# Start stage of a two-layer adaptive FFN kernel: factor merges in six groups, eight zero products, x loads by SyncE, lists reordered

## The reference, cut to what matters

```python
hidden_i = jnp.einsum('bsd,fd->bsf', x, wi)
hidden_i += ALPHA * jnp.einsum('bsr,fr->bsf', jnp.einsum('bsd,rd->bsr', x, common_wi_a), common_wi_b)
hidden_i += _expert_lora(x, expert_ids, experts_wi_a, experts_wi_b)
hidden_i = jax.nn.relu(hidden_i)
hidden_o = jnp.einsum('bsf,df->bsd', hidden_i, wo)
...
for r in range(R):                       # four rounds, R = 4
    logits = flat @ Wg[r] + bg[r]        # top 2 of 4 experts, softmax weights cw
    hmid = jax.nn.gelu(jnp.einsum('nh,ehf->enf', flat, W1) + b1[:, None, :])
    y = jnp.einsum('enf,efh->enh', hmid, W2) + b2[:, None, :]
    cur = cur + jnp.einsum('ne,enh->nh', cw, y).reshape(b, s, h)
x = x + ...
```

## Time and profile before

| what | us |
|---|---|
| median of 3 runs (485.28 to 486.13) | 485.58 |
| the profiled execution | 486.61 |
| its span, first to last instruction | 484.80 |
| its mean granted TensorE clock, as a share of full speed | 0.996 |

### The profile page before, as it was taken

The page is one execution under the profiler, slowest core; times in us unless marked ns, Lnnn a source line. Parts: engine busy times, 40 slices in busy tenths (PEclk is TensorE's granted clock), DMA queues, the critical chain, the costliest instruction groups (busy, mean ns, idle before and its releaser), DMA issues.

```text
span 484.8 us, 7478 instructions
## 1 busy us (share of the span) xinstructions
PE 477.9 (99%) x2270; PEld 397.0 (82%) x2270; DVE 387.7 (80%) x641; ACT 393.9 (81%) x542; POOL 118.7 (24%) x102
## 2 busy tenths in 40 slices
PE   7999999999999999999999999999999999999997
PEld 7998888888888888888888888888888887888885
DVE  4789899999879898988898898889897758554343
ACT  3799988888888888988888888888888888697653
POOL 5796212121212112121222121231313144400000
PEclk9999999999999999999999999999999999999999
DMA  7702702020201102020202012120202000000001
GB/s 209 215 5 88 266 18 89 2 87 3 87 11 76 71 16 87 0 87 0 87 0 87 11 76 82 49 89 0 87 2 87 2 0 0 1 0 1 0 22 69
DMA packets 6986, 26.30 MB, mean 54 GB/s; under 512 B 2226, under 2 KB 2610, under 8 KB 4786
## 3 DMA queue, kind: packets, MB, share of 16 engines
q1 hardware_dynamic: 5826, 21.20, 12.1%
q0 software_dynamic: 528, 3.67, 2.2%
q10 hardware_dynamic: 608, 1.11, 0.8%
HBM read 24.81 MB, written 1.18 MB: 54 GB/s over the span
## 4 chain that ended last, share of the span: by engine, by line
PE 96%; DMA 2%; SPq 1%; issue 0%; DVE 0%
PE bank L505 34%; PE bank L506 34%; PE bank L509 26%; DMA stage<-lora_all 2%; PE bank L594 1%; PE bank L595 1%; PE bank L527 1%; SPq L244 0%; SPq L247 0%; PE bank L540 0%; PE bank L524 0%; SPq L257 0%; DVE x L1276 0%; SPq L345 0%; SPq L344 0%
## 5 line engine op out<-in xcount | busy, mean ns | idle before, releaser
L812 ACT ACTIVATE act_out<-bank,vec 128x512 f32<-128x512 f32 x256 | 165.4, 682 | 41.8 <-PE bank L509 32.6
L1115 DVE TENSOR_TENSOR hid_lo<-act_out,hid_hi 128x1024 fp32r<-128x1024 f32 x128 | 156.6, 1243 | 33.3 <-ACT hid_hi L817 33.2
L817 ACT ACTIVATE hid_hi<-act_out 128x1024 fp32r<-128x1024 f32 x128 | 135.9, 1062 | 8.0 <-PE bank L509 0.2
L468 POOL TENSOR_TENSOR cur<-cur,prod 128x512 f32<-128x512 f32 x48 | 64.9, 1352 | 238.4 <-DVE prod L1126 237.9
L505 PE MATMUL bank<-hid_hi,moe_hi 128*128 128x512 f32 x256 | 99.9, 390 | 0.0
L509 PE MATMUL bank<-hid_hi,moe_lo 128*128 128x512 f32 x256 | 99.7, 390 | 0.0
L505 PE MATMUL bank<-xhi,moe_hi 128*128 128x512 f32 x256 | 99.7, 390 | 0.0
L506 PE MATMUL bank<-hid_lo,moe_hi 128*128 128x512 f32 x256 | 99.7, 389 | 0.0
L506 PE MATMUL bank<-xlo,moe_hi 128*128 128x512 f32 x256 | 99.6, 389 | 0.0
L509 PE MATMUL bank<-xhi,moe_lo 128*128 128x512 f32 x256 | 99.6, 389 | 0.0
L505 PEld LDWEIGHTS bank<-hid_hi,moe_hi 128*128 128x128 f32 x256 | 48.1, 188 | 11.3 <-issue 0.2
(11 more groups left out here) (126 smaller groups left out, 569.9 us busy)
## 6 DMA issues: line engine op xcount, KB each, us to landing
cw_all<-cw_dram SPq DMA_DIRECT2D x16, 1024.0 KB, 4.6
stage<-ffn_w POOLq DMA_DIRECT2D x1, 2304.0 KB, 8.5
cw_all<-moe_w SPq DMA_DIRECT2D x4, 512.0 KB, 10.3
stage<-lora_all SPq DMA_DIRECT2D x5, 160.0 KB, 7.1
x<-x_t POOLq DMA_DIRECT2D x3, 256.0 KB, 7.0
out_t<-x SPq DMA_DIRECT2D x3, 256.0 KB, 2.5
cur<-cond_base ACTq DMA_DIRECT2D x2, 256.0 KB, 3.1
stage<-ffn_w POOLq DMA_DIRECT2D x1, 512.0 KB, 3.8
```

Of the source, the lines that this page charges most:

```text
L468: pool.tensor_tensor(cur[:, c, :], cur[:, c, :], prod[:, s % 2, :], ALU.add).then_inc(add_done, 1)
L812: act.activation(act_out[:, f // 2, f % 2, :], bank[:, f, :], ACT.Gelu_apprx_tanh, bias=vec[:, V_B1 + e * FC + f:V_B1 + e * FC + f + 1]).t ...
L817: act.activation(hid_hi[:, s % 2, 2 * pr:2 * pr + 2, :], act_out[:, pr, :, :], ACT.Copy)\
L1115: dve.tensor_tensor(hid_lo[:, s % 2, 2 * pr:2 * pr + 2, :], act_out[:, pr, :, :], hid_hi[:, s % 2, 2 * pr:2 * pr + 2, :].bitcast(F32), ALU ...
```

## The change

Nothing that is computed changes. Seven things do:

1. The 16 merges stand in six groups instead of seven: sizes 2, 2, 3, 3, 3, 3 instead of 2, 2, 2, 2, 3, 3, 2. All groups behind the second use banks 5 to 7; banks 2 and 3 are no longer used for merges.
2. `KEEP_WARM` is 8 instead of 2.
3. x chunks 1, 2 and 3 are issued by SP instead of POOL: chunk 1 behind the factors of batch 2, chunks 2 and 3 behind those of batch 7, ahead of `moe_w`.
4. The sum, high part and low part of merge (0, 0) are made in two halves of 256 columns, with semaphores of their own, and `cond_hidden(0)` waits for each half.
5. The low parts of conditioned chunks 2 and 3 are made by POOL from `cur` instead of by DVE from PSUM; `cond_out(6)` waits for the copy of chunk 2 only.
6. `split_gate` and `x0_low(2)` move from DVE to POOL.
7. The lists of PE, ACT, DVE and POOL stand in a new order.

```diff
 MERGE_GROUPS = (((0, 0), (1, 0)),
                 ((0, 1), (1, 1)),
-                ((2, 0), (3, 0)),
-                ((2, 1), (3, 1)),
-                ((4, 0), (5, 0), (4, 1)),
-                ((6, 0), (7, 0), (5, 1)),
-                ((6, 1), (7, 1)))
+                ((2, 0), (3, 0), (2, 1)),
+                ((4, 0), (5, 0), (3, 1)),
+                ((6, 0), (4, 1), (5, 1)),
+                ((7, 0), (6, 1), (7, 1)))
-MERGE_BANKS = (6, 7, 4, 5, 2, 3, 6, 7, 5, 6, 7, 5, 6, 7, 5, 6)
+MERGE_BANKS = (6, 7, 5, 4, 6, 7, 5, 6, 7, 5, 6, 7, 5, 6, 7, 5)
-WARM, KEEP_WARM = 13, 2
+WARM, KEEP_WARM = 13, 8
             expert_load(sp, 2, expert)
+            x_load(sp, 1)
             for b in (4, 5, 6, 7):
                 lora_load(sp, b)
+            x_load(sp, 2)
+            x_load(sp, 3)
...
-            pool.wait_ge(first_out_in[1], 16)
-            for c in range(1, CHUNKS):
-                x_load(pool, c)
+            def conditioned_low(c):
+                pool.wait_ge(cond_cur, c + 1)
+                pool.tensor_tensor(xlo[:, c, :], cur[:, c, :], xhi[:, c, :].bitcast(F32), ALU.subtract)\
+                    .then_inc(xs_done, 1)
...
                 for f in range(FC):
+                    if b == 0 and f % 2 == 0:
+                        pe.wait_ge(first_lo_done, f // 2 + 1)
...
                     pe.wait_ge(merge_free, summed_in(COND, len(MERGED)))
+                elif b == PER_CHUNK * (CHUNKS - 1):
+                    pe.wait_ge(cond_cur, c)
                 elif b % PER_CHUNK == 0:
                     pe.wait_ge(xs_done, c)
...
             merge_group(2)
-            merge_group(3)
             cond_hidden(0)
             cond_hidden(1)
-            merge_group(4)
+            merge_group(3)
             cond_out(0)
             cond_hidden(2)
-            merge_group(5)
+            merge_group(4)
             cond_out(1)
             cond_hidden(3)
             cond_hidden(4)
-            merge_group(6)
+            merge_group(5)
             cond_out(2)
             cond_out(3)
+            cond_hidden(5)
             first_logits(0)
-            cond_hidden(5)
             cond_hidden(6)
             cond_out(4)
             cond_out(5)
+            cond_hidden(7)
+            cond_out(6)
+            expert_in(0, 0, 0, (0,))
             first_logits(1)
...
+            def first_sum():
+
+                dve.wait_ge(base_in[0], 16)
+                dve.wait_ge(merge_done, MERGED.index((0, 0)) + 1)
+                for half, summed in zip(halves, (first_sum_done, merge_free)):
+                    dve.scalar_tensor_tensor(merged(0, 0)[:, half], bank[:, merge_bank(MERGED.index((0, 0))), half], COND_ALPHA,
+                                             base[:, 0, half], ALU.mult, ALU.add).then_inc(summed, 1)
```

More of the change, by code:

```diff
@@ L219, in adaln_ffn @@
         out_done = sem("out_done")
+        halves = [slice(0, F // 2), slice(F // 2, F)]
         block = ctx.enter_context(nc.Block())
@@ L447, in _ @@
             merged_low(6, 1)
+            moe_low(0)
+            merged_low(7, 1)
             moe_low(4)
-            merged_low(7, 1)
             moe_low(1)
@@ L452, in _ @@
             moe_low(2)
+            pool.wait_ge(cond_cur, CHUNKS)
+            for i in range(2):
+                pool.memset(prod[:, i, 0:1], 0.0).then_inc(add_done, 1)
             moe_low(6)
+            conditioned_low(2)
             moe_low(3)
+            conditioned_low(3)
             moe_low(7)
@@ L697, in _ @@
             cond_out(5)
+            cond_hidden(7)
+            cond_out(6)
+            expert_in(0, 0, 0, (0,))
             first_logits(1)
-            cond_hidden(7)
-            expert_in(0, 0, 0, (0,))
             expert_in(0, 0, 0, (1,))
-            cond_out(6)
+            cond_out(7)
             expert_in(0, 0, 0, (2,))
-            cond_out(7)
+            expert_in(0, 0, 0, (3,))
             merge_lang()
-            expert_in(0, 0, 0, (3,))
             with pe.Fori(0, ROUNDS - 1) as rnd:
@@ L798, in merged_high, with first_merged_high @@
                 act.activation(mer_hi[:, b % AHEAD, kind, :], merged(b, kind), ACT.Copy).then_inc(mer_hi_done, 1)
+            def first_merged_high():
+                for half, summed, done in zip(halves, (first_sum_done, merge_free), (first_hi_done, mer_hi_done)):
+                    act.wait_ge(summed, 1)
+                    act.activation(mer_hi[:, 0, 0, half], merged(0, 0)[:, half], ACT.Copy).then_inc(done, 1)
             def lang_high(half):
@@ L899, in _ @@
             base_load(act, 1)
+            x0_high(0)
             lora_load(act, 3)
-            x0_high(0)
-            merged_high(0, 0)
+            first_merged_high()
             merged_high(1, 0)
+            x0_high(1)
             merged_high(0, 1)
+            merged_high(2, 0)
+            relu_high(0)
+            merged_high(2, 1)
             merged_high(1, 1)
-            x0_high(1)
-            relu_high(0)
-            merged_high(2, 0)
-            merged_high(2, 1)
-            merged_high(3, 1)
-            relu_high(1)
-            merged_high(4, 0)
             merged_high(3, 0)
             x0_high(2)
+            relu_high(1)
+            merged_high(5, 0)
+            merged_high(3, 1)
+            merged_high(4, 0)
+            x0_high(3)
             relu_high(2)
+            moe_high(0)
+            conditioned_high(0)
+            conditioned_copy(0)
             merged_high(4, 1)
-            conditioned_high(0)
-            x0_high(3)
-            conditioned_copy(0)
-            moe_high(0)
             relu_high(3)
-            merged_high(5, 0)
+            merged_high(5, 1)
             moe_high(4)
+            moe_high(1)
             merged_high(6, 0)
+            moe_high(5)
             merged_high(7, 0)
@@ L1222, in _ @@
             merged_sum(2, 1)
+            relu_low(0)
+            merged_sum(5, 0)
             merged_sum(3, 1)
-            relu_low(0)
             merged_sum(4, 0)
+            relu_low(1)
             merged_sum(4, 1)
-            merged_sum(5, 0)
-            relu_low(1)
-            x0_low(2)
             relu_low(2)
-            merged_sum(7, 0)
             merged_sum(6, 0)
-            x0_low(3)
+            merged_sum(5, 1)
             conditioned_low(0)
             relu_low(3)
+            merged_sum(7, 0)
+            x0_low(3)
             merged_sum(6, 1)
-            merged_sum(7, 1)
-            merged_sum(5, 1)
             relu_low(4)
             conditioned_low(1)
+            merged_sum(7, 1)
+            relu_low(5)
             gate_logits(0, 0)
-            relu_low(5)
+            relu_low(6)
             gate_order(0, 0)
-            relu_low(6)
+            relu_low(7)
             gate_choice(0, 0)
-            conditioned_low(2)
             gate_gap(0, 0)
-            relu_low(7)
             gate_logits(1, 0)
```

89 lines of the change are left out of this document (41 added, 48 removed).

## The result

The changed kernel is slower, by less than half a per cent: 487.18 us (486.69 to 488.17, 8 runs) against 485.38 us of the kernel before (485.23 to 486.13, 8 runs). The ratio is 1.004, with 1.003 to 1.005 as its 95% interval. The forecast was 483.5 us and faster, with 482.7 to 485.3 as the range: the wrong sign, and the time lies outside the range. The profiled execution took 488.17 us with a span of 486.4 us and a mean granted clock of 1.000.

A forecast was written before the change was run, and what follows sets the result against it. PE bounds the kernel, with time to win only ahead of the loop: 2.4 us gained less 0.3 us of wait is 2.1 us, so the median goes from 485.58 to 483.5 us, range 482.7 to 485.3.

The forecast's parts named there:

- POOL: POOL's list ahead of the loop: four gate operations and three more low parts fit, with a reserve of 1.0 us.
- from there on both programs have the same work: Rival: batch 5's factors land at 16.2, as late as before, and nothing later differs: 485.9 us, chance 0.12.
- The clock's fall: PE at half clock from 11.28 to 14.48, behind its first wait: 16 records, 1.5 us; expected to stay at 2.4 GHz.
- The second wait of 0.53 us: PE's wait ahead of merge group 4 for batch 5's factors, landing at 15.76; 0.3 us expected to be left.
- The zero products' own time: PE ahead of group 2: twelve more records take 1.3 to 1.7 us, done between 9.1 and 9.4, costing nothing.
- Batch 3's factors: ACT's load that group 2 waits for: issue 0.2 us later, taken as even; group 2 at 9.5, bounds 9.0 to 9.9.
- Batch 5's factors and x: Factors issued by SP at 7.8 land at 13.8, leaving PE 0.3 us of wait; x chunk 2 just in time.
- the warning that the prediction took from the Trainium skill's rule: Transfers from different engines interleave on the same 16 engines, so moving x to SP only adds 0.45 us of issue.
- the rival of a late x chunk 2: ACT's `relu_high(1)` stands behind x chunk 2: late by about a microsecond, chance 0.13; by three, 0.07.
- the other two: Rivals at the start: clock falls all the same, 484.6 us, chance 0.15; transfer as late as before, 485.9, 0.12.
- The sum up to the loop: PE's path from group 2 at 9.53 to the loop at 41.6 against 44.02: gain 2.4 us if nothing is late.
- The low part beside DVE: One POOL low part takes 1.28 us, up to 1.75 us beside DVE.

The follow-up runs named there:

- experiment 1: Changed kernel with POOL's wait for the conditioned copies and its two memsets moved behind `moe_low(3)`: 485.34 us, ratio 0.9999 against the kernel before.
- experiment 4: Changed kernel with two zero products behind merge group 1 instead of eight: 488.83 us, ratio 1.0061 against the kernel before.
- experiment 5: Kernel before with eight zero products instead of two, nothing else: 485.19 us, ratio 0.9998.
- experiment 2: Kernel before with POOL's wait (on `xs_done`) and two memsets moved ahead of `moe_low(6)`, `(3)` and `(7)`: 486.81 us, ratio 1.004.
- experiment 6: Kernel before with x chunks 1 to 3 issued by SP instead of POOL, nothing else: 485.6 us, ratio 1.0012.
- experiment 9: Experiment 1 with ACT's load of batch 3's factors issued ahead of `x0_high(0)`: 485.35 us, ratio 1.0003 against the kernel before.
- experiment 3: Changed kernel with POOL's wait and two memsets one place later, behind `moe_low(6)`: 486.07 us, ratio 1.0016 against the kernel before.
- experiment 7: Kernel before with both x chunks 1 to 3 issued by SP and eight zero products instead of two: 485.1 us, ratio 0.9991.
- experiment 8: Changed kernel with conditioned low parts 2 and 3 back on DVE, POOL's wait and memsets behind `moe_low(7)`: 490.84 us, ratio 1.0124 against the kernel before.
- experiment 10: Experiment 9 with five zero products behind merge group 1 instead of eight: 485.74 us, ratio 1.0023 against the kernel before.

## Why the prediction was wrong

The forecast missed by 3.7 us. One half of it is a wait that the prediction didn't see, 1.84 us; the other half is a gain of 2.1 us that was taken from one execution and isn't in the median.

**The step that failed** stands under *POOL*: "`conditioned_low` on POOL feeds only the loop", and "its first user on PE is at 36 us", with which the prediction left POOL's list. It counted what POOL's operations cost and when PE wants the results up to the loop. It did not read the wait that went with them, `pool.wait_ge(cond_cur, CHUNKS)` behind `moe_low(2)`, which came with part 7, the new lists. It asked what is queued behind a waiting instruction for ACT and x chunk 2, and didn't ask it here: `moe_low(3)`, which frees the slot of `cw_all`, then SP's broadcast, DVE's `prod`, its `hid_lo`, and PE. And it ended its sum at the loop's entry, taking the loop as the same in both ("from there on both programs have the same work", as it says of a rival). The cost of the missed wait is 1.84 us (experiment 1); none of the rivals was it.

**The clock's fall** (1.5 us): the mechanism was right, and experiment 4 shows it worth 1.5 to 1.65 us in the changed program. Its size for this comparison was wrong, since it was read from one execution. That execution lay 1.03 us above the median; the prediction noted this, subtracted the gain and then shifted the result down by the same 1.03, as if the fall were in the median too. With the fall in 2 of 67 executions the term for the median is about 0, and the zeros alone measured 0.1 us (experiment 5). The second wait of 0.53 us, behind a landing of 8.4 us, had the same fault: experiment 5 has no such wait, experiment 2 one of 0.26. The mean clock of 0.996 beside the 486.61 us was the sign.

**The zero products' own time** was put at 1.3 to 1.7 us for the added ones, ending at 9.1 to 9.4. Eight products take 2.05 us in the row above; in the profiled execution of experiment 1 they start at 7.39, and the next group at 9.70 waits 0.26 us. The term holds.

**Batch 3's factors** were taken as even, group 2 at 9.5 with 9.0 to 9.9 as bounds. This was mis-sized. In the three profiled executions with x on POOL's queue (before and experiments 5 and 2) group 2 starts at 9.53, 9.65 and 8.88. In the nine with x on SP's queue it starts at 9.63 to 11.58, their middle at 10.49. Behind the issue of the load (at 5.0 in the three) it starts 3.9 to 4.65 us later in the three, and 4.35 to 5.6 us later in the nine. A likely cause is x chunk 1, which SP issues at 5.3 to 5.4, beside this load, while POOL's x, which the prediction weighed against it, was issued at 5.9 to 6.5; that is argued from these times and no run shows it by itself. Single executions scatter here by about a microsecond, so the middle is worth more than any one of them.

**Batch 5's factors and x.** The factors were put at 13.8 with a wait of 0.3 us; group 3 starts at 15.74 and, in experiment 1, at 13.85, with no wait in either. Their landing, 4.5 us at the longest, is even better than the 6.0 the prediction took. What is issued later did spare the earlier loads, but the load that now has x chunk 1 beside it is batch 3's, the one that sets the start of group 2. So the warning that the prediction took from the Trainium skill's rule was right in the sum: by experiment 6 the move of x alone wins nothing (ratio 1.0012). In the profiled execution `relu_high(1)` did not wait for x chunk 2: `x0_high(2)` runs at 16.89 without idle time, and the rival of a late x chunk 2 fell. So did the other two: the clock stayed up in all eight executions of the changed kernel, and no transfer was late behind SP's queue.

**The sum up to the loop.** It ended at 44.02, which in the kernel before is a piece of `expert_in` behind `merge_lang`; this was taken as the entry, with 2.8 us of pieces and `merge_lang` counted ahead of it. Against that the sum left out the seams between blocks. Experiment 1 enters at 42.69, from group 2 at 9.70: 32.99 us where the sum had 32.1, so the seams are 0.9 us. The check "from 15.90 gives 44.0" agreed by luck: one piece of 0.7 us too many stood in it for about as much of seams. What counts is the path from group 2's start to the first mark. In the new order it is 41.27 or 41.28 us in four executions (changed 52.85 - 11.58, experiment 1 50.98 - 9.70, experiment 9 51.60 - 10.32, experiment 3 51.98 - 10.70). In the old order it is 41.52 in experiment 7, where nothing disturbs it, and 42.17 in experiment 5, where `x0_high(1)` stood 1.26 us idle for x chunk 1 and PE 0.48 us ahead of `cond_out(0)`. The new order is therefore some 0.25 us shorter by itself, up to 0.9 with the waits that it spares, and group 2 starts about a microsecond later (9.53 and 10.49 are the middles above): together nothing, which is what experiment 1 measures.

**The low part beside DVE** was put at 1.28 to 1.75 us. At the loop's entry it takes up to 2.33 us (46.95 above), while DVE's `hid_lo`, which began at 46.91, kept to 1.20. Where POOL's began first (49.24, 1.29 us), DVE's `hid_lo` of 49.65 took 1.97 us, against 1.22 in the kernel before at the same place. This widened the lateness: two of the three operations ahead of the slot's release ran at the longer time. The Trainium skill has a rule for it, in "SBUF — State Buffer", section "Who interferes with whom": GpSimd's only ports are the second pair of VectorE's, and whoever holds the pair locks the other out. The trace agrees with it here, in both directions: one of the two keeps its time and the other is stretched (1.20 beside 2.33 us, 1.29 beside 1.97 us).

**What stays open.** Where the other four executions of experiment 2 (486.74 to 487.38 us) lost a further 1.5 to 2.1 us, since only the lowest was profiled; what part 3 costs by itself at POOL's first load; and why group 2's factors scatter by a microsecond between executions.

## What to carry to other kernels

When an instruction list is rewritten, look for the waits that moved as well as for the work, and follow each to whatever is queued behind it, through the slots that this frees, past the end of the stage that the change is about: here a memset's wait held back an expert's low part, that a buffer slot, that a broadcast, and so PE in the next stage. Set two marks on the bounding engine in a part that the change leaves alone, and compare their distance in both traces; it finds a one-time loss that busy shares and waits of half a microsecond hide. A loss ahead of the first mark escapes it, as the 0.9 us of experiment 2 would have: measure the way to the first mark too. And ask whether a stall read from one profiled execution is in the median too: a mean clock or a time that stands off the other runs says it may not be.

## What the hardware showed

- The fall of TensorE's clock behind a pause at the start is a matter of chance between executions of one program: 2 of 67 in the kernel before (two zero products), 4 of 11 with x on SP's queue, 5 of 6 in the new order with two zeros, 2 of 7 with five, and none of 62 in the kernels with eight (the changed one and experiments 1, 3, 5, 7 and 9; experiment 8's fall lies elsewhere, behind its wait at 39.7). The executions with the fall took 1.1 to 2.7 us more than the median of the others of the same kernel.
- x chunk 0, issued by ACT at 1.26 or 1.27 in every kernel, was ready at 4.45, 4.59, 5.15, 5.23 and 6.31 us in the five profiled executions in which `x0_high(0)` waited for it first (experiments 8, 1, 4 and 3, and the changed kernel).
- A GpSimd subtraction of 512 columns takes 1.3 us undisturbed and VectorE's `hid_lo` of 1024 columns, with both inputs in SBUF, 1.2. Where the two overlapped, one kept its time and the other took longer: GpSimd's 2.0 to 2.9 us, or VectorE's 1.7 to 2.2. With VectorE starting half a microsecond behind, it was GpSimd's in experiments 1 and 9 (2.87 us) and VectorE's in experiment 10 (1.86). Beside `relu_low`, whose first input is a PSUM bank, neither was stretched: six low parts in 7.55 us (36.61 in the kernel before) and 1.23 us.
- GpSimd's first issue of a load took 0.86 us, whatever the load was (x or `ffn_w`), and a later one 0.54 to 0.58.
